# First experts of a four-layer block on one Trainium2 core: second layer in three rounded matmuls, gates applied to finished sums, transfers reordered

## What is computed

```python
scores = jnp.einsum('bsd,ed->bse', x, Wg)
topk_scores, topk_idx = jax.lax.top_k(scores, k)          # k = 2 of 8
topk_probs = jax.nn.softmax(topk_scores, axis=-1)
h1 = jnp.einsum('bsd,efd->bsef', x, W1)
h2 = jnp.einsum('bsd,efd->bsef', x, W2)
hidden = jax.nn.silu(h1) * h2                             # 256 wide for each expert
expert_out = jnp.einsum('bsef,edf->bsed', hidden, W3)
onehot = jax.nn.one_hot(topk_idx, scores.shape[-1], dtype=x.dtype)
gating = jnp.einsum('bsk,bske->bse', topk_probs, onehot)
return jnp.einsum('bse,bsed->bsd', gating, expert_out)
```

## Time and profile before

| | |
|---|---|
| median of 3 executions | 1627.1 us (1621.42 to 1632.26) |
| profiled execution | 1632.3 us, span 1630.4 us |
| busy: PE, DVE, ACT, POOL | 1494.1, 1378.2, 1148.6, 163.2 us |
| causal attention | to about 302 us |
| first experts | about 302 to 705 us |
| full attention | about 705 to 1350 us |
| second experts | about 1350 us to the end |

### The profile page before, as it was taken

One profiled execution on the slowest core, in us unless ns is written; L12 is line 12 of the kernel. 1 busy time (PEld: TensorE's weight loads), 2 busy tenths in 40 slices (PEclk: granted clock), 3 DMA queues, 4 the chain that ended last, 5 costly groups with the idle time before them and its releaser, 6 DMA issues.

```text
span 1630.4 us, 31489 instructions
## 1 busy us (share of the span) xinstructions
PE 1494.1 (92%) x11072; PEld 761.5 (47%) x11072; DVE 1378.2 (85%) x2375; ACT 1148.6 (70%) x1782; POOL 163.2 (10%) x231
## 2 busy tenths in 40 slices
PE   7988989599999999969999999999999998999996
PEld 4333333266656656623333333333333333777775
DVE  4899999668778778787999999999999973788886
ACT  4999999433332333215899999999999986777775
POOL 0000000101101101010000000000000001234333
PEclk9999999799999999975899999999999997999999
DMA  6636432221234422210211111111111110211211
GB/s 195 206 110 174 125 94 84 78 76 49 71 106 126 125 92 80 64 40 2 88 42 36 36 36 36 49 42 43 36 37 36 36 31 28 68 54 62 74 54 40
DMA packets 71022, 116.72 MB, mean 72 GB/s; under 512 B 23808, under 2 KB 33920, under 8 KB 70272
## 3 DMA queue, kind: packets, MB, share of 16 engines
q1 hardware_dynamic: 70912, 115.21, 23.2%
HBM read 73.49 MB, written 41.16 MB: 70 GB/s over the span
## 4 chain that ended last, share of the span: by engine, by line
PE 42%; DVE 23%; issue 14%; ACT 12%; DMA 4%; POOL 2%; SPq 1%; DVEq 0%; ACTq 0%; POOLq 0%
PE full_o L713 11%; DVE negmax_h L803 9%; PE max_pair L684 9%; ACT cprobs L486 7%; PE hid_pair L1025 6%; PE score L698 3%; PE causal_o L458 3%; PE bank L1118 3%; DVE hid L1431 2%; PE triple L442 2%; PE bank L1130 2%; DVE lin_u L1427 1%; POOL e_sm L1501 1%; DVE st L1265 1%; DMA k_scr<-qk_hi 1%
## 5 line engine op out<-in xcount | busy, mean ns | idle before, releaser
L766 ACT ACTIVATE probs<-score 128x512 f32<-128x512 f32 x1024 | 546.7, 596 | 95.0 <-PE score L698 74.7
L803 DVE TENSOR_REDUCE negmax_h<-max_pair 128x2 f32<-128x1024 f32 x512 | 589.0, 1216 | 28.6 <-PE max_pair L684 28.5
L713 PE MATMUL full_o<-probs,v_st 128*32 128x256 f32 x4096 | 340.7, 406 | 17.3 <-ACT o_sb L774 17.2
L698 PE MATMUL score<-q_st,k_st 32*128 32x512 f32 x1024 | 320.4, 512 | 2.6 <-ACT probs L766 2.6
L684 PE MATMUL max_pair<-k_st,q_st 32*128 32x512 f32 x1024 | 266.8, 519 | 11.3 <-DVE negmax_h L803 9.8
L486 ACT ACTIVATE cprobs<-triple 128x1536 f32<-128x1536 f32 x192 | 258.4, 1713 | 4.8 <-PE triple L442 4.8
L684 PEld LDWEIGHTS max_pair<-k_st,q_st 32*128 32x128 f32 x1024 | 98.6, 190 | 237.9 <-DVE negmax_h L803 178.1
L1227 ACT ACTIVATE act_s<-hid_pair 128x512 f32<-128x512 f32 x128 | 76.4, 597 | 189.2 <-PE hid_pair L1025 189.1
L1025 PE MATMUL hid_pair<-x_hi,w_hi 128*128 128x512 f32 x384 | 194.9, 508 | 0.6 <-ACT act_s L1231 0.6
L516 DVE TENSOR_SCALAR cprobs<-cprobs 128x1536 f32<-128x1536 f32 (+6 forms) x272 | 160.6, 618 | 3.1 <-ACT cprobs L486 3.1
L458 PE MATMUL causal_o<-cprobs,v_st 128*32 128x512 f32 (+3 forms) x1536 | 155.6, 501 | 2.2 <-DVE cprobs L516 2.2
(11 more groups left out here) (147 smaller groups left out, 1598.7 us busy)
## 6 DMA issues: line engine op xcount, KB each, us to landing
gate_all<-gate_scr SPq DMA_DIRECT2D x48, 512.0 KB, 4.8
o_scr<-o_sb SPq DMA_DIRECT2D x64, 256.0 KB, 2.1
k_st<-k_scr SPq DMA_DIRECT2D x64, 128.0 KB, 2.8
q_st<-q_scr SPq DMA_DIRECT2D x128, 64.0 KB, 2.5
k_st<-k_scr SPq DMA_DIRECT2D x64, 96.0 KB
q_st<-q_scr SPq DMA_DIRECT2D x64, 96.0 KB
q_scr<-qk_hi SPq DMA_DIRECT2D x18, 256.0 KB, 5.2
k_scr<-qk_hi SPq DMA_DIRECT2D x18, 256.0 KB, 4.6
```

What stands on the lines that cost most here:

```text
L698: nc.tensor.matmul(sbank[L.score_bank(e)][:, :], k_st[p][rows, kt * P:(kt + 1) * P], q_st[p][rows, q0:q0 + w], start=True, stop=True, tile ...
L713: last = nc.tensor.matmul(full_o[SLOT * j:SLOT * (j + 1), cols], v_st[p][:, kt, j, :], probs[s % NP][:, j, cols], start=(kt == 0 and part ...
L766: nc.scalar.activation(probs[s % NP][:, L.HEADS[j], :], sbank[L.score_bank(e)][:, :], ACT.Exp, scale=SCALE).then_inc(L.exp_done, 1)
L803: nc.vector.tensor_reduce(negmax_h[:, qt // TPC, half, heads[0]:heads[1] + 1:2, qt % TPC], ring[slot][:, :, :], AXX, ALU.max, negate=True) ...
```

## The change

- The hidden rows are no longer multiplied with gates. DVE multiplies the linear bank with the Silu (`hid`), ACT copies it to `hid_hi`, DVE takes the remainder (`dve_lower0`), and `pe_product` issues three rounded matmuls with `w3_hi` and `w3_lo`. These two parts of w3 are made once, by ACT and DVE, ahead of the stage.
- The two steps of an expert add up in one of two banks. DVE multiplies the finished sum with the expert's gates (`dve_weigh`, eight a chunk), POOL adds the results (`pool_add`, seven a chunk).
- The hidden matmuls run three steps ahead (`h_lead` 1 to 3), and ACT and DVE have the work beside two steps later (`LATE` 0 to 2).
- POOL takes from DVE the product `ot`, the remainders `x_lo` and both `qk_lo`; ACT takes the copies to `x_tm` and `v_all`. The Exp of the gate goes from ACT to POOL, as a power of e.
- SP issues `sp_load_o` ahead of gates and stores. The first chunk's gates are made in its own steps, not before the first hidden matmul.
- Eight pairs of maxima, before six, stand beside the last back, from step 1 on.
- In the second experts the weighing stands one step earlier (`WEIGH_AT` 2 to 1), and POOL's two adds of the last experts stand together ahead of the root for the front.

```diff
-HB = (0, 8)
-LATE = (0, 4)
+HB = (4, 8)
+LATE = (2, 4)
...
-    BESIDE_BACK = {6: (0, 1), 7: (2, 3), 8: (4, 5)}
+    BESIDE_BACK = {1: (0,), 2: (1,), 4: (2, 3), 7: (4,), 8: (5, 6), 9: (7,)}
...
-        for pl, steps in ((plan[0], (2, 4, 6, 7, 8, 9, 1, 1, 3, 4, None, 5, 7, 9)),
+        for pl, steps in ((plan[0], (2, 4, 6, 7, 8, 9, 1, 1, 3, 4, None, 5, 8, 10)),
...
-        GATES_AT, WEIGH_AT = 1, 2
+        GATES_AT, WEIGH_AT = 1, 1
...
-        h_banks, h_lead = [2, 4], [1, 5]
+        h_banks, h_lead = [2, 4], [3, 5]
...
-        lower = [[], hid_lo + qk_hi]
+        lower = [[qk_hi[2], qk_hi[3], qk_lo[2], qk_lo[3]], hid_lo + qk_hi]
+        y_part = [o_sb[0], y_tmp]
...
             if layer == 0:
-                pe.wait_ge(st.u_done, c * SPC + n + 1)
+                pe.wait_ge(st.m_done, c * SPC + n + 1)
...
-        def pe_product(pe, st, c, n):
-
-            pe.wait_ge(st.hid_ready, c * SPC + n + 1)
-            nc.tensor.matmul(bank[0][:, :], w3[:, n, :], hid[n % 2][:, :], start=(n == 0),
-                             stop=(n == SPC - 1)).then_inc(st.y_done, 1)
...
+        def pe_product(pe, st, c, n, layer):
+
+            per = SPC // n_exp[layer]
             e, f = n // per, n % per
             if f == 0:
-                wait_used(pe, st.y_used, c * E1 + e - 1)
+                wait_used(pe, st.y_used, c * n_exp[layer] + e - 1)
             pe.wait_ge(st.hid_ready, c * SPC + n + 1)
...
+            for a, (w, x) in enumerate(((up, hi), (down, hi), (up, lo))):
+                last = nc.tensor.matmul(y_bank[e % 2], w, x, start=(f == 0 and a == 0),
                                         stop=(f == per - 1 and a == 2))
...
+        def act_upper(act, st, m):
+
+            act.wait_ge(st.m_done, NS + m + 1)
+            wait_used(act, st.y_done, m - HB[0] + 1)
+            nc.scalar.activation(hid_hi[m % HB[0]][:, :], hid[m % 2][:, :], ACT.Copy).then_inc(st.hi_done, 1)
...
+                    act.wait_ge(st.m_done, c * SPC + n + 1)
                     nc.scalar.activation(act_s[n % 2][:, :], hbank[n % 2], ACT.Silu).then_inc(st.s_done, 1)
+                    if c + n > 0:
+                        act_upper(act, st, c * SPC + n - 1)
+                    if c == 0 and n == 4:
+                        act_save_gates(act, st, 0)
...
-            if layer == 0:
-                act.wait_ge(st.y_done, (c + 1) * SPC)
-                nc.scalar.activation(y_sb[:, :], bank[0][:, :], ACT.Copy).then_inc(st.y_saved, 1)
...
+            if layer == 0:
+                nc.vector.tensor_tensor(to, y_bank[e % 2], gate, ALU.mult).then_inc(st.y_used, 1)
...
+        def dve_lower0(dve, st, m):
+
+            dve.wait_ge(st.hi_done, m + 1)
+            wait_used(dve, st.y_done, m - HB[0] + 1)
+            nc.vector.tensor_tensor(lower[0][m % HB[0]][:, :].bitcast(F32R), hid[m % 2][:, :],
+                                    hid_hi[m % HB[0]][:, :].bitcast(F32), ALU.subtract).then_inc(st.hid_ready, 1)
...
-                    nc.vector.tensor_tensor(lin_u[n % 2][:, :], hbank[2 + n % 2], gate_all[e // 2][:, e % 2, :],
-                                            ALU.mult).then_inc(st.u_done, 1)
-                    dve.wait_ge(st.u_done, NS + c * SPC + n + 1)
-                    dve.wait_ge(st.s_done, h_banks[layer] + c * SPC + n + 1)
-                    nc.vector.tensor_tensor(hid[n % 2][:, :], act_s[n % 2][:, :], lin_u[n % 2][:, :],
-                                            ALU.mult).then_inc(st.hid_ready, 1)
+                    m = c * SPC + n
+                    dve.wait_ge(st.s_done, h_banks[0] + m + 1)
+                    wait_used(dve, st.hid_ready, m - 1)
+                    nc.vector.tensor_tensor(hid[n % 2][:, :], hbank[2 + n % 2], act_s[n % 2][:, :],
+                                            ALU.mult).then_inc(st.m_done, 1)
+                    if m > 0:
+                        dve_lower0(dve, st, m - 1)
...
+                if layer == 0 and n % 2 == 0 and (n > 2 or back is not None):
+                    dve_weigh(dve, st, c if n > 2 else back, (n // 2 - 2) % E0, 0)
...
+                dve.wait_ge(st.w3_upper, 1)
+                nc.vector.tensor_tensor(w3_lo[:, :, :], w3[:, :, :], w3_hi[:, :, :].bitcast(F32),
+                                        ALU.subtract).then_inc(st.w3_lower, 1)
...
+        def pool_gate_exp0(pool, st, f):
+
+            pool.wait_ge(st.gate_pre, f + 1)
+            nc.gpsimd.tensor_tensor(p12[:, 1, :], euler[:, 0:TPC], lead[:, :], ALU.pow).then_inc(st.gate_exp, 1)
...
+                if c + 3 <= LAST:
+                    sp_load_o(sp, st, layers[0], f, f // 2, f % 2)
                 if c + 2 <= LAST:
                     keep_gates(st, c + 2)
                     load_gates(st, c + 2, (0, 1))
                 if c >= 0:
                     store_chunk(c)
-                if c + 3 <= LAST:
-                    sp_load_o(sp, st, layers[0], f, f // 2, f % 2)
```

214 lines of the change are left out of this document (126 added, 88 removed).

## The result

The changed kernel takes 1606.8 us (median; 1602.8 to 1611.3), the kernel before on the same chip 1629.5: a ratio of 0.988, 95% interval 0.985 to 0.990. It is 12 us above the forecast of 1595. The span of the profiled execution went from 1630.4 to 1609.5 us, by 20.9, where the forecast's sum was 32; that execution, of 1611.3 us, is the longest of the four measured. Experiment 7 changes only the second experts, so its profile shows the same program for the first experts a second time.

A forecast was written before the change was run, and what follows sets the result against it. PE was read as nearly full, waiting 4.5 us a chunk; afterwards VectorE's norms and choice, then PE, set the period. Terms -17, -3, -3, -1, -8 sum to -32: 1600 profiled, 1595 median (1580 to 1608, chance 0.57).

The forecast's parts named there:

- PE's floor, 40.8: First experts: least time PE needs a chunk, 33.3 us of steps plus 7.5 of shorter work beside them.
- That wait goes: First experts' queue: the front's load lands half a chunk early; if late, it costs part of 4.5 us a chunk.
- has room: First experts: ACT, busy 16.5 us of 48, can take the added copies, reaching 29 even with 18 of them.
- VectorE's remainders: First experts: remainders behind a weighing wait about 0.7 us for GpSimd's add; mean 0.85 to 0.95 us, unblocked 0.68.
- The walk, 45.4: First experts' chunk period: VectorE's steps 3 to 7 take 17.4 us, PE's way onward 28.0; taken as 45.2, -17 in all.
- PE's turn of x_out waits for the end of this: First experts: PE's x_out turn waits for VectorE's 17.4 us of norms and router's choice; PE cannot get ahead before it.
- Start: -3: Start of the first experts: the stall moves to weighing 0, with a few shorter steps after; -3 us (0 to -8).
- Transition -1: From the first experts' last sum to the first scores: earlier maxima against added weighing, adds and gap; -1 us (0 to -4).
- Second experts: -8: Second experts: weighing a step earlier and both adds before rstd save half of 13.4 us of PE's waits; 0 to -13.
- Rival 1: First experts: blocking falls into VectorE's idle time and PE's floor is reached; period 42, 1566 us in all, chance 0.20.
- Rival 2: Most is given back: blocked remainders and GpSimd's serial queue show; period 46.8, 1614 us in all, chance 0.16.
- Rival 3: Slower: each GpSimd operation holds VectorE its whole 1.27 us, needing 56 a chunk; 1660 us in all, chance 0.07.

The follow-up runs named there:

- Experiment 7: Changed kernel with only the second experts' part undone (weighings a step later, one late GpSimd sum behind the root): 1609.4 us, 0.991 of the kernel before.
- experiment 8: Changed kernel with only the queue's order undone, the coming front's load again behind gates and stores: 1643.5 us, 1.009 of the kernel before.
- experiment 1: Changed kernel with ACT's copy of x_out to x_tm one step later, behind its copies to xt and x_hi: 1607.0 us, 0.987 of the kernel before.
- experiment 9: Changed kernel with PE's xs turn, router and x_out turn behind their steps' hidden blocks, and ACT's x_tm copy later: 1594.3 us, 0.980 of the kernel before.
- Experiment 4: Changed kernel with ten of GpSimd's thirteen large operations a chunk cut to 8 of 512 columns: 1603.3 us, 0.986 of the kernel before.
- 10: Changed kernel with eight useless matmuls on PE ahead of its wait for xs, once a chunk with both neighbours: 1607.1 us, 0.988 of the kernel before.
- 2: Changed kernel with VectorE's front normalisation one step earlier, exchanged with the residual of the chunk behind: 1631.4 us, 1.002 of the kernel before.
- 3: Changed kernel with VectorE's front normalisation and residual exchanged, and ACT's copy to x_tm later as well: 1625.7 us, 1.000 of the kernel before.
- 6: Changed kernel with VectorE and ACT one step behind PE's plan instead of two in the first experts: 1633.1 us, 1.003 of the kernel before.
- 12: Turns-behind-hidden-blocks version with x_out's turn and q, k, v a step later, GpSimd's rotary work spread between sums: 1608.0 us, 0.988 of the kernel before.

## Why the prediction was right in sign and too large

**PE's floor, 40.8.** The steps are as forecast: hidden block 1.37 to 1.39, product 0.69. The short things beside them were an estimate of 2.3 for router and turns; the chain shows 0.44 + 0.44 + 0.66 + 1.03 + about 0.5. The floor is 33.3 + 8.3 = 41.6, 0.8 above the forecast's. The same 0.8 was missing from the floor before, so of the 4.5 us a chunk read there as PE waiting at most 3.7 were; the waits that the trace of before names for PE are 15.0 us from 340 to 660 us, 2.3 a chunk.

**The queue.** "That wait goes": right; there is no wait for o_rcp in the stage. Its price was wrong. The 4.5 us of waits a chunk were to be what a late load costs at most; with the new order of the engines a late load costs 7 us a chunk (experiment 8), since the division is now ahead of GpSimd's sums.

**ACT "has room".** It has, 156 us busy of 320, and the table reloads are gone. But room was read from busy time, and the place of the new copies in ACT's order was costed at nothing. The copy to x_tm waits for x_out with xt, x_hi and a Silu behind it, 21.7 us in seven chunks. Lifting it alone gives nothing that is seen (experiment 1), together with PE's order 1.6 to 2.0 us a chunk (experiment 9).

**VectorE's remainders.** The forecast gave 0.85 to 0.95 us on average and 0.7 for a blocked one; measured 0.92 and 0.72 at 505.75 (1.32 against 0.60). The mechanism and its size were right. The walk, though, had three blocked remainders in steps 3 to 7, and the chunk read closely has one that counts. By the Trainium skill, SBUF — State Buffer, section Who interferes with whom, two SBUF inputs are what collides. The trace agrees for the remainder beside a sum (1.32 at 505.75); beside GpSimd's small root of 128x4 no delay is seen (0.68 at 513.38, the root from 512.80 to 513.84, and GpSimd's spans are rough). Experiment 4 shows that taking ten of thirteen such neighbours away is worth 0.9 to 1.2 us a chunk in all.

**The walk, 45.4, taken as 45.2.** From product 3 (505.14) to the end of the choice (522.68) are 17.5 us; the forecast had 17.4. That is a hit by two errors that cancel: 1.4 less work, mostly blocked remainders, and 1.6 more for the wait for ACT at 519.47. From PE's turn of x_out (523.52) to the next product 3 (551.93) are 28.4; the forecast had 28.0. Between the two lie 0.84 us in which PE finishes a product at the lower clock. Sum 46.8. So of the 1.6 us by which this period was missed, 0.84 is that low clock ahead of the turn, 0.4 the part behind it (the floor's short things), 0.1 the walk and 0.2 the step from 45.4 down to 45.2. This is the account of one period with a late fall; those with an early one are 0.7 to 0.9 shorter, and the one with a fall of 10 us is 2.2 longer. The term of the sum that was mis-sized is this period: 2.9 us less were forecast, 1.2 came (1.6 in experiment 7's execution).

**"PE's turn of x_out waits for the end of this; before that it cannot get ahead."** Wrong in its place. PE waited 14.8 us at the turn of xs and 1.5 at the turn of x_out. The turn of xs stands ahead of hidden 7 and product 4, and needs what VectorE does behind its remainder for product 4. Ready matmuls stood behind it, which the walk did not have; experiment 9, which lets them run, gets 1.6 to 2.0 us a chunk where the change to ACT alone (experiment 1) gets nothing that is seen.

**Clock.** The forecast assumed no change in PE's clock. Inside the stage there was one: it fell once in each chunk; a late fall costs 0.65 us (experiments 7 and 10) to 1.2 (experiment 4), an early one nothing that is seen. The forecast had set two bounds that would make it wrong, a period above 47 and over 5 us a chunk of PE waiting for VectorE; the mean stays below the first (one period of 48.97 does not), and all of PE's named waits are 3.1 us a chunk. Behind the stage the low stretch was shorter in the profiles:

```profile
720.00:770.00 50.00, 42.86 (x214) 14.53 (x214) 39.73 (x38) 19.01 (x36) 0.83 (x4) 0.50 0.09 27
...
720.00:770.00 50.00, 47.33 (x346) 16.67 (x344) 38.08 (x37) 33.19 (x63) 0.84 (x4) 0.64 0.14 49
...
720.00:770.00 50.00, 48.78 (x481) 18.67 (x479) 45.51 (x45) 43.34 (x84) 1.65 (x7) 0.92 0.23 72
...
720.00:770.00 50.00, 47.67 (x392) 18.07 (x392) 41.99 (x40) 37.44 (x71) 0.83 (x4) 0.78 0.18 58
```

These rows are before, after, experiment 9 and experiment 7, clock 0.50, 0.64, 0.92 and 0.78. The stage ends at another time in each, so the end of the low stretch is better counted from the first scores: it comes about 40, 30 and 9 us behind them. From the first scores to the second experts they take 634.5, 631.7 and 625.1 us with the same work. So 2.8 of the change's 20.9 and 6.6 of experiment 9's 14.9 lie there. But this is not shown to be the edits' doing: experiment 7, whose program is after's up to the second experts, takes 625.9 us there, with the low stretch ending 17 us behind the first scores. That is 5.8 us between two executions of the same code. The other kernels take 625.0 to 633.8, most of them near 625 or near 631.5. Why PE comes back to 2.4 GHz earlier in some was not tested.

**Start: -3.** 2.5 up to the first rotary projection. Weighing 0 was forecast for 333 and product 4 for 339.5: 333.06 and 339.37. **Last chunk -3:** 4.4 between the last two rotary projections. **Transition -1:** 3.7 from there to the first scores, part of it the last chunk's.

**Second experts: -8, measured -1.5 (experiment 7: 2.6).** The waits named did go: 16.7 us in all to 3.8. New ones came in their place, for xs 6.8, for mv 3.7, for gts 3.0 instead of 0.7. All of PE's waits from 1350 us on are 20.5 before (without one of 1.9 at a score, which is the attention's) and 20.6 after. The step that failed is taking half of the waits removed as time gained, on an engine that waits for the same VectorE a little later.

**The rivals.** Rival 1 (PE's floor reached, period 42): no; the smallest single period in any run is 44.8. Rival 2 (most is given back, period 46.8, 1614): its period is nearly what came (46.85, and 46.48 in experiment 7), by another mechanism, and with some 8 us more gained around the chunks. Rival 3 (VectorE held by GpSimd): no; VectorE is busy 41 us a chunk, not 56. The sum of the six periods was to be -17 and is about -7; with the second experts' 6.5 that is 16.5 too much, against which 5 more were gained at the end of the stage and in the attention behind it, of which the 2.8 in the attention are luck of the executions as far as is known.

## What to carry to other kernels

Room on an engine is no place in its order: for every operation that a change puts on another engine, ask what it waits for and what stands behind it there, and for every wait of the bound engine whether ready work stands behind that wait. Here moving three short operations of TensorE behind matmuls that were ready, with one copy of ScalarE a step later, was worth more (1.6 to 2.0 us a chunk) than nearly emptying ten of thirteen operations of GpSimd (0.9 to 1.2). A wait that is removed counts as time only when the engine has no second wait on the same producer; sum all of its waits before and after. And a wait that is moved in a loop between three engines may come back larger: four of seven reorderings (2, 3, 6, and 12 against 9) cost 14 to 26 us. Last, profile the same code twice before a difference of a profile is given to an edit: here two executions differ by 0.4 us in each chunk and by 5.8 us behind the stage.
